# Where the value products are written and which engine takes which small step, in a one-core attention and two-expert layer on Trainium2

## The reference

```python
h = _layernorm(x) * (1 + ca) + sa
x = x + ga * attn(h, w_dq, w_uq, w_dkv, w_ukv, w_out)      # softmax(q k^T / 4 + causal mask) v
h = _layernorm(x) * (1 + cb) + sb
scores = softmax(h @ Wg.T); top = argmax(scores)             # two experts
out0 = gelu(h @ W0a.T + b0a) @ W0b.T + b0b                   # exact gelu
out1 = relu(h @ W1a.T + b1a) @ W1b.T + b1b
x = x + gb * where(top == 0, out0, out1)
```

## Time and profile before

| | us |
|---|---|
| median of 3 runs | 596.92 (595.57 to 600.63) |
| profiled execution | 593.84, its span 592.1 |
| PE busy | 515.4 (87% of the span) |
| DVE busy | 480.8 (81%) |
| ACT busy | 366.5 (62%) |
| POOL busy | 311.9 (53%) |

### The profile page before, as it was taken

How to read it: one execution, slowest core, us unless ns; L and a number is a source line. 1 busy time by engine, 2 the same in 40 slices (tenths; PEclk the granted TensorE clock), 3 DMA queues, 4 the chain that set the end, 5 groups by cost and what they waited for, 6 DMA issues and landing times.

```text
span 592.1 us, 14257 instructions
## 1 busy us (share of the span) xinstructions
PE 515.4 (87%) x4912; PEld 446.2 (75%) x4912; DVE 480.8 (81%) x949; ACT 366.5 (62%) x521; POOL 311.9 (53%) x300
## 2 busy tenths in 40 slices
PE   4534685989999999999999999999999999999974
PEld 4424463788888988888888888788988898888874
DVE  3538163779999899989898989999899999887573
ACT  1524464858585866667676858585766667676320
POOL 6235232455656665755646565656665665552441
PEclk9856598899999999999999999999999999999998
DMA  8835453262707080716244351708080615210100
GB/s 246 206 46 76 50 74 75 52 95 37 128 18 145 2 161 3 121 42 90 71 68 93 50 111 31 130 7 154 0 152 13 108 39 91 55 39 2 37 19 18
DMA packets 43802, 43.74 MB, mean 74 GB/s; under 512 B 5344, under 2 KB 40800, under 8 KB 43760
## 3 DMA queue, kind: packets, MB, share of 16 engines
q1 hardware_dynamic: 43760, 43.19, 39.1%
HBM read 13.39 MB, written 4.23 MB: 30 GB/s over the span
## 4 chain that ended last, share of the span: by engine, by line
PE 49%; DVE 19%; DMA 10%; issue 9%; SPq 5%; POOL 3%; ACT 3%; DVEq 0%; POOLq 0%; ACTq 0%
DMA qs<-parts_q 8%; PE ps_s L382 6%; DVE mx L933 6%; PE ps_t L401 5%; PE ps_o L419 3%; PE ps_a L333 3%; PE ps_t L405 3%; SPq L282 3%; PE ps_a L334 3%; PE ps_a L335 3%; PE ps_c L333 3%; PE ps_c L335 2%; PE ps_c L334 2%; PE ps_o L333 2%; POOL xs L1186 2%
## 5 line engine op out<-in xcount | busy, mean ns | idle before, releaser
L794 ACT ACTIVATE score_rows<-ps_s 128x1024 f32<-128x1024 f32 x96 | 98.8, 1030 | 79.3 <-PE ps_s L382 66.2
L1246 POOL TENSOR_SCALAR_AFFINE_SELECT score_rows<-score_rows 128x512 f32<-128x512 f32 (+1 forms) x96 | 80.0, 834 | 110.4 <-ACT score_rows L794 109.8
L933 DVE TENSOR_REDUCE mx<-score_rows 128x4 f32<-128x1024 f32 (+1 forms) x96 | 114.6, 1210 | 5.7 <-POOL score_rows L1246 5.5
L806 ACT ACTIVATE p<-ps_t 128x1024 f32<-128x1024 f32 x96 | 98.5, 1026 | 17.9 <-PE ps_t L405 17.3
L382 PE MATMUL ps_s<-ks,qs 96*128 96x256 bf16 (+1 forms) x512 | 63.3, 260 | 33.2 <-DMA qs<-parts_q 29.7
L382 PEld LDWEIGHTS ps_s<-ks,qs 96*128 96x128 bf16 x512 | 37.0, 103 | 47.9 <-DMA qs<-parts_q 23.2
L1186 POOL TENSOR_TENSOR xs<-z,xs 128x512 f32<-128x512 f32 (+1 forms) x16 | 34.9, 2182 | 68.7 <-DVE z L1022 68.7
L401 PE MATMUL ps_t<-qs,ks 99*128 99x256 bf16 (+1 forms) x512 | 61.1, 254 | 11.0 <-DMA qs<-mx_rows 10.3
L401 PEld LDWEIGHTS ps_t<-qs,ks 99*128 99x128 bf16 x512 | 38.8, 101 | 17.5 <-DMA qs<-mx_rows 6.3
L405 PE MATMUL ps_t<-past_b,ident_b 128*128 128x256 bf16 (+1 forms) x192 | 46.0, 322 | 0.0
L1234 POOL TENSOR_TENSOR hid_lo<-hid,hid_hi 128x512 fp32r<-128x512 f32 x32 | 42.8, 1350 | 4.8 <-DVE hid_hi L1092 4.8
(11 more groups left out here) (166 smaller groups left out, 1631.4 us busy)
## 6 DMA issues: line engine op xcount, KB each, us to landing
qs<-parts_q SPq DMA_DIRECT2D x96, 128.0 KB, 4.0
ks<-parts_k SPq DMA_DIRECT2D x96, 128.0 KB, 4.7
xs<-x SPq DMA_DIRECT2D x16, 256.0 KB, 4.1
gates<-gates_scratch SPq DMA_DIRECT2D x16, 256.0 KB, 4.5
out<-xs SPq DMA_DIRECT2D x16, 256.0 KB, 2.9
p<-wmod SPq DMA_DIRECT2D x1, 1024.0 KB, 6.7
p<-waT SPq DMA_DIRECT2D x1, 1024.0 KB, 9.1
p<-wmod SPq DMA_DIRECT2D x1, 512.0 KB, 5.9
```

Source lines behind the costliest of these rows:

```text
L794: act.activation(score_rows[c % 2][:], ps_s[:], ACT.Copy).then_inc(scores_out, 1)
L806: act.activation((p0, p1)[tile][:, h0:h0 + n, :], ps_t[:].rearrange("p (h s) -> p h s", h=n), ACT.Exp, scale=SCALE).then_inc(exp_done, 1)
L933: dve.tensor_reduce(dst, score_rows[c % 2][:].rearrange("p (h k) -> p h k", h=n), AX_X, ALU.max).then_inc(max_done, 1)
L1246: pool.affine_select(out=diag, in_=diag, compare_op=ALU.is_ge, fill=NEG, base=0, pattern=[[0, n], [-1, P]], channel_multiplier=1).then_inc ...
```

## The change

- `values` computes all four groups in one piece, into `ps_t` (each group 256 columns), after the last exponentials of the batch; `values_copy` reads it there in two halves, both at the end of ACT's step (before: the second half was second in the next step). The first `st_chunk` of the next batch waits for these copies. The memset of `ps_o` at the start goes. `turn_values(at(3), 0)` now names other users of `ps_o`.
- `choose_expert` reads the first logit straight from PSUM and copies only the second; `second` comes from a comparison "less than" of its own instead of from `first`.
- `relu` moves from DVE to ACT, with the same waits; `relu(at(4), 2)` stands ahead of `v_copy`, `attn_hi` and the first `exponentials`, `relu(at(4), 3)` ahead of the first `scores_copy`.
- On SP `stack_q(_, 2)` moves from the head of the next step to behind `stack_k(at(0), 0)`, and `load_maxima` goes ahead of `load_gates`.
- POOL gets a wait for the end of `split_maxima`, `leave_to_split(at(1))`, between `q_third` and `k_third`.

The diff, cut to its core:

```diff
@@ sync step
-                stack_q(at(1), 2)
                 stack_q(at(0), 0)
                 stack_q(at(0), 1)
                 stack_k(at(0), 0)
+                stack_q(at(0), 2)
+                load_maxima(at(1))
                 load_gates(at(2))
-                load_maxima(at(1))
                 stack_k(at(0), 1)
@@ tensor
-                "GT": ((logit_rows_ready, 1, 1),), "GX": ((logits_ready, 1, 1),),
+                "GT": ((logit_rows_ready, 1, 1),), "GX": ((choice_ready, 2, 2),),
...
                 if c == 0:
                     pe.wait_ge(maxrows_in, 16 * (b.n + 1))
+                    wait(pe, o_ready, 2 * b.n)
...
+            def values(b):
+
+                if b.off:
+                    return
+                pe.wait_ge(v_ready, b.n + 1)
+                pe.wait_ge(exp_done, CH * (b.n + 1))
+                for g in range(4):
+                    for n in range(4):
+                        h = 4 * g + n
+                        dst = ps_t[32 * n:32 * n + HD + 1, g * S:(g + 1) * S]
+                        pe.matmul(dst, v[b.parity][:, 0, h, :], p0[:, h, :], start=True, stop=False)
+                        mm = pe.matmul(dst[:, P:S], v[b.parity][:, 1, h, :], p1[:, h, :], start=False, stop=True)
+                    if g % 2 == 1:
+                        mm.then_inc(pv_done, 1)
...
                 st_chunk(at(2), 5)
-                values(at(2), 0, ("DN0", at(4)), ("UP3", at(4)), ("V", at(1)))
                 s_chunk(at(1), 5)
-                values(at(2), 1)
                 expand_k(at(0), ("CKV", at(0)))
                 up(at(3), 0, ("Q", at(0)), ("T2", at(3)))
-                values(at(2), 2, ("PVa", at(2)))
-                values(at(2), 3)
+                values(at(2))
                 up(at(3), 1, ("DN1", at(4)), ("T1", at(0)))
@@ scalar
+            def relu(b, u):
+
+                if b.off:
+                    return
+                act.wait_ge(up_done, 4 * b.n + u + 1)
+                act.wait_ge(lo_gelu_ready, 2 * b.n + u - 1)
+                act.wait_ge(hid_hi_ready, 4 * b.n + u - 1)
+                for n in range(2):
+                    ins = act.activation(hid32[:, u - 2, n, :], BANK[f"UP{u}"][:, n * S:(n + 1) * S], ACT.Relu,
+                                         bias=bias_a[:, 2 * u + n:2 * u + n + 1])
+                ins.then_inc(relu_done, 1)
...
                 gelu(at(4), 0)
-                values_copy(at(3), 1)
                 maxima_rows(at(2))
                 gelu(at(4), 1)
+                relu(at(4), 2)
                 v_copy(at(1))
                 attn_hi(at(3))
                 exponentials(at(2), 0)
+                relu(at(4), 3)
                 scores_copy(at(1), 0)
...
                 scores_copy(at(1), 5)
+                k_first(at(0))
                 values_copy(at(2), 0)
-                k_first(at(0))
+                values_copy(at(2), 1)
@@ vector
-                dve.tensor_copy(logits[:], BANK["GX"][:, 0:2 * TT].rearrange("p (t e) -> p t e", e=2)).then_inc(logits_ready, 1)
+                pair = BANK["GX"][:, 0:2 * TT].rearrange("p (t e) -> p t e", e=2)
+                dve.tensor_copy(logits[:, :, 1], pair[:, :, 1]).then_inc(logits_ready, 1)
                 dve.wait_ge(logits_ready, b.n + 1)
-                dve.tensor_tensor(first[b.parity][:], logits[:, :, 0], logits[:, :, 1], ALU.is_ge).then_inc(first_ready, 1)
-                dve.wait_ge(first_ready, b.n + 1)
-                dve.tensor_scalar(second[b.parity][:], first[b.parity][:], -1.0, 1.0, ALU.mult, ALU.add).then_inc(choice_ready, 1)
+                dve.tensor_tensor(first[b.parity][:], pair[:, :, 0], logits[:, :, 1], ALU.is_ge).then_inc(choice_ready, 1)
+                dve.tensor_tensor(second[b.parity][:], pair[:, :, 0], logits[:, :, 1], ALU.is_lt).then_inc(choice_ready, 1)
@@ gpsimd
+            def leave_to_split(b):
+
+                if b.off:
+                    return
+                pool.wait_ge(max_split, 4 * (b.n + 1))
...
                 q_third(at(0))
+                leave_to_split(at(1))
                 k_third(at(0))
                 hidden_low(at(3), 0)
```

More of the change, by code:

```diff
@@ L186, in block_kernel @@
             "z2_ready t2_done g32_ready g_hi_ready g_lo_ready".split())
-        gate_done, logit_rows_ready, gate_turned, logits_ready, first_ready, choice_ready = (sem(n) for n in
-            "gate_done logit_rows_ready gate_turned logits_ready first_ready choice_ready".split())
+        gate_done, logit_rows_ready, gate_turned, logits_ready, choice_ready = (sem(n) for n in
+            "gate_done logit_rows_ready gate_turned logits_ready choice_ready".split())
         up_done, gelu_done, relu_done, hid_hi_ready, lo_gelu_ready, lo_relu_ready = (sem(n) for n in
@@ L210, in block_kernel @@
         BANK = dict(T1=ps_a, Q=ps_c, CKV=ps_b, K=ps_b, V=ps_o, MT=ps_c, OT0=ps_o, OT1=ps_b, AT=ps_b, OP=ps_c, T2=ps_c,
-                    GT=ps_a, GX=ps_b, UP0=ps_c, UP1=ps_a, UP2=ps_c, UP3=ps_o, DN0=ps_o, DN1=ps_a, PVa=ps_o, PVb=ps_o)
+                    GT=ps_a, GX=ps_b, UP0=ps_c, UP1=ps_a, UP2=ps_c, UP3=ps_o, DN0=ps_o, DN1=ps_a)
         LAGS = 4
@@ L406, in st_chunk @@
                 mm.then_inc(st_done, 1)
-            def values(b, g, *users):
+            def values(b):
                 if b.off:
                     return
[L412 to L421, removed]
+                pe.wait_ge(v_ready, b.n + 1)
[8 more added lines that the diff above has]
+                        mm.then_inc(pv_done, 1)
             def turn_values(b, t, *users):
@@ L603, in _ @@
             pe.wait_ge(consts_ready, 6)
-            pe.wait_ge(blank, 4)
+            pe.wait_ge(blank, 3)
             pe.wait_ge(z1_ready, 1)
@@ L625, in step @@
                 st_chunk(at(2), 0)
-                up(at(4), 3, ("V", at(1)), ("OT0", at(3)), ("PVb", at(3)), ("PVa", at(3)), ("DN0", at(5)))
+                up(at(4), 3, ("V", at(1)), ("OT0", at(3)), ("DN0", at(5)))
                 project_out(at(3), ("UP2", at(4)), ("MT", at(2)))
@@ L685, in values_copy @@
                     return
-                act.wait_ge(pv_done, 4 * b.n + 2 * half + 2)
+                act.wait_ge(pv_done, 2 * b.n + half + 1)
                 wait(act, ot_done, 2 * b.n)
-                act.activation(oT[:, 2 * half:2 * half + 2, :], BANK["PVa"][:].rearrange("p (g s) -> p g s", g=2), ACT.Copy).then_inc(o_ready, 1)
+                act.activation(oT[:, 2 * half:2 * half + 2, :], ps_t[:, half * 512:(half + 1) * 512].rearrange("p (g s) -> p g s", g=2), ACT.Copy).then_inc(o_ready, 1)
             def second_expert(b, t):
@@ L694, in second_expert @@
                 act.wait_ge(dn_done, 4 * b.n + 2 * t + 2)
-                act.wait_ge(choice_ready, b.n + 1)
+                act.wait_ge(choice_ready, 2 * (b.n + 1))
                 wait(act, out_ready, b.n)
@@ L763, in v_copy @@
                 act.wait_ge(v_done, b.n + 1)
-                wait(act, pv_done, 4 * (b.n - 1))
+                wait(act, pv_done, 2 * (b.n - 1))
                 act.activation(v[b.parity][:, :, :, 0:HD], BANK["V"][:].rearrange("p (t h e) -> p t h e", t=TT, h=NH), ACT.Copy).then_inc(v_ready, 1)
@@ L799, in exponentials @@
                 act.wait_ge(st_done, CH * b.n + c + 1)
-                wait(act, pv_done, 4 * (b.n - 1) + (2, 1, 2, 4, 3, 4)[c])
+                wait(act, pv_done, 2 * (b.n - 1) + (1, 1, 1, 2, 2, 2)[c])
                 if b.first and c == 0:
@@ L915, in _ @@
                 dve.memset(v[n][:, :, :, HD:HD + 1], 1.0).then_inc(blank, 1)
-            dve.memset(ps_o[:], 0.0).then_inc(blank, 1)
             stats(Batch(0, 0, NB), 0)
@@ L1123, in step @@
                 first_stats(at(0))
-                relu(at(4), 2)
                 attn_low(at(3))
                 hidden_high(at(4), 2)
-                relu(at(4), 3)
                 gate_copy(at(4))
```

17 lines of the change are left out of this document (3 added, 14 removed).

## The result

The changed kernel takes 624.75 us in the median of four runs (621.07 to 626.86), the kernel before 596.9: 4.5% slower, ratio 1.045 with a 95% interval of 1.038 to 1.052. The forecast was 597.4 us and the range ended at 607.

What follows compares the result with a forecast made beforehand. Two nearly equal loops were taken to bound a step: PE's work, and split, maxima rows, SP's list, DMA. Regular steps +1.2, third step +0.6, last step −1.3 gave +0.5 us: 597.4 us from 596.92, range 586 to 607.

Steps and rivals of the forecast that it cites:

- 0.4 us later: ACT, regular step: maxima rows are copied only after second value copy, table load and gelu, so their DMA starts 0.4 us later.
- PE takes over from there: Regular step: DVE, relieved of about 2.9 us, bounds no more; PE's 0.2 us wait for the split goes.
- 0.2 us sooner for the last issue: SP's list: behind the maxima one 0.58 us issue leaves and the gates' 0.36 us enters, so the last issue comes sooner.
- The landing: Time from the last part's issue to its arrival for `s_chunk` 0: taken as 3.65 us, possibly 0.7 us later.
- Rival C: Slower: the late k part lands 0.7 us later than a q part would; 607 us, chance 0.06.
- Third step: Filling: PE's 5.10 us idling for the maxima goes, but `s_chunk` 0 comes about 0.6 us later; +0.6 us.
- Last step: Emptying: relu on ACT starts sooner, so the gate's copy on DVE is ready at about 577.0; −1.3 us.
- rival D: Slower: the relus on ACT need a table load each, two more of 1.28 us; 628 us, chance 0.02.
- rival B: Slower: ACT held behind `relu` 2, which waits for GpSimd's `hidden_low`; 604 to 611 us, chance 0.20.
- lower bound: DVE, new choice: `second` was bounded by 0.17 and 1.20 us; 0.2 us was taken, a gain of 1.0 us.
- rival A: Faster: DVE's room pulls work before the split forward, SP's last DMA lands sooner; 583 to 589 us, chance 0.27.
- The merged bursts: PE: four value groups in one piece take 2.90 instead of 3.05 us, a gain of 0.15 us.

Runs made afterwards that it cites:

- gelu_first: The changed kernel with gelu 0 moved to the end of ACT's step before, ahead of the two value copies: 603.9 us, ratio 1.014.
- sp_q_only: The kernel before with only the third part of q issued behind the first of k, gates still ahead of the maxima: 606.3 us, ratio 1.022.
- sp_only: The kernel before with SP's whole new list alone (third q part moved, maxima ahead of gates): 609.0 us, ratio 1.020.
- relu_back: The changed kernel with relu back on DVE in its old places: 624.75 us, ratio 1.047.
- hold_only: The kernel before with GpSimd's wait for the split between q_third and k_third alone: 594.3 us, ratio 0.995.
- choice_relu: The kernel before with relu on ACT and the choice read from PSUM, all else as before: 594.9 us, ratio 0.996.
- loads_last_relief: The kernel before with the last k and q parts issued ahead of the store and the load of x, relu on ACT, new choice: 582.9 us, ratio 0.981.
- sp_maxima_only: The kernel before with load_maxima ahead of load_gates and nothing else: 627.4 us, ratio 1.055.

## Why the prediction was wrong

**What failed first is a dependency, not a size.** The working followed ACT correctly from the second copy over the table load and the gelu to the maxima rows, and gave the maxima "0.4 us later". It has the gelu end 2.8 us after the values, and it ended 2.9 us after them (320.92 and 323.83). But the prediction has PE's transposition done by then ("PE takes over from there"), although its bank is that of `up` 0 and must be read by that same gelu. Measured, PE stood idle for 1.37 us and began `turn_maxima` 0.14 us after the gelu's end. By the prediction's own numbers the transposition could not start before 310.9, 0.8 us behind the row. PE's idling, with a term of its own in each step, was never in the sum. It also pushes back everything behind: `turn_values`, `up` 2, and the maxima's DMA. One line moved (gelu_first) takes 21 of the 28 us back.

**SP's list** was the second step that failed. "0.2 us sooner for the last issue" was right: counted from `turn_maxima`, the last part is issued 5.03 us later instead of 5.28 in the mean of ten steps. The landing was mis-sized. I took 3.65 us, the shortest of those ten steps before, whose mean is 3.96; in the changed kernel it was 4.84 in the mean and 5.39 in the step shown. Rival C named this mechanism, with 0.7 us more for the landing, and the means differ by 0.9. I gave it a chance of 0.06. Two things were not in the sum at all: the maxima land later behind the early q part, which PE waits for in gelu_first and sp_q_only, and 256 KB of gates between the maxima and the last part delay that part. sp_only put the price of the whole list at 12.8 us.

**The size of the step.** Of the 1.89 us that a step grew, 1.1 are PE's wait ahead of `turn_maxima` and 0.6 lie between it and `s_chunk` 0. The rest is the balance of the lower clock and of PE's slightly shorter work.

**The clock** was not in the sum. It stayed at the upper level in the regular steps before, with waits of at most 1.5 us. In the changed kernel it fell in four of the eleven steps. Each of these took 1.4 to 1.7 us more than the step of 33.6 us that had a wait of 2.09 us and kept its clock.

**Third step.** The 5.10 us wait was expected to go and `s_chunk` 0 to come 0.6 us later. The SP rows and PE rows of that step, first of the kernel before where the earlier trace rows lacks them:

```profile
83.62 1.83 SPq L282 DMA_DIRECT2D ks<-parts_k  x3
...
90.80 0.78 SPq L271 DMA_DIRECT2D qs<-mx_rows  x1
...
94.31 0.55 SPq L282 DMA_DIRECT2D qs<-parts_q  x1
```

```profile
98.57 0.62 PE L382 MATMUL ps_s<-ks,qs 96*128 96x128 bf16 x8 [0.63 <-DMA qs<-parts_q]
```

And of the changed kernel:

```profile
85.29 1.83 SPq L282 DMA_DIRECT2D ks<-parts_k  x3
...
87.81 0.77 SPq L271 DMA_DIRECT2D qs<-mx_rows  x1
88.62 0.42 SPq L260 DMA_DIRECT2D gates_scratch<-gates  x1
93.97 0.36 SPq L263 DMA_DIRECT2D gates<-gates_scratch  x1
...
96.42 0.55 SPq L282 DMA_DIRECT2D ks<-parts_k  x1
```

```profile
93.82 1.04 PE L402 MATMUL ps_t<-qs,ks 99*128 99x128 bf16 x8 [3.75 <-DMA qs<-mx_rows]
...
101.84 1.01 PE L382 MATMUL ps_s<-ks,qs 96*128 96x128 bf16 x8 [3.57 <-issue]
```

The wait for the maxima shrank only to 3.75 us. The maxima were issued 3.0 us sooner (87.81 against 90.80), but behind the q part PE could use them 6.0 us after their issue instead of 3.3. `s_chunk` 0 came at 101.84 instead of 98.57, 3.3 us later. Of these, 1.7 were lost before (the first k parts go at 85.29 instead of 83.62). The other 1.6 stand against the 0.6 of the sum. Counted from those k parts the round trip began 1.45 us later (2.1 in the sum), and it took 0.45 us longer. The last issue behind it came 1.46 us sooner (1.4 in the sum). The landing, of which the sum took no account here, took 5.4 us instead of 4.3.

**Last step.** −1.3 us was expected. The idle time ahead of `turn_gate` fell from 1.86 to 1.07 us, −0.8:

```profile
607.75 0.25 PE L559 MATMUL ps_b<-ident,logit_rows 2*128 2x2 f32 x2 [1.07 <-DVE logit_rows L1066]
```

**What was right.** relu on ACT is as long as on DVE, 471 and 472 ns beside 479, without a table load of its own (rival D is refuted):

```profile
L802 ACT ACTIVATE hid<-ps_c,bias_a 128x256 f32<-128x256 f32 x20 | 8.4, 471 | 20.5 <-PE ps_c L335 12.3 <-POOL hid_lo L1236 8.2
```

It did wait behind GpSimd's `hidden_low` (8.2 us, in four of the steps) and held the v copy, as drawn in the prediction, but PE had other waits by then, and relu_back shows that the place costs nothing here; rival B is refuted as the cause. The Trainium skill (ScalarE: Activation LUTs, Rules for kernel authors) speaks for VectorE with a figure for bf16. For float32 from PSUM the rows show no difference in length. The new choice took 150 ns for `second`, just under the lower bound. That bound's row was misread: at 541.48 GpSimd was not idle but in a 128x2 instruction of 0.70 us from 541.03 on. The instruction took the same 0.17 us at 516.26 and 580.02, with GpSimd idle, so the number stands. DVE was busy for 84% of the regular steps (268.81 of 320 us), near the 85% forecast. GpSimd's wait was free (hold_only). That DVE's relief would shorten nothing while SP's chain closes the step was right as well (choice_relu, 0.996), and the part of rival A that DVE's room shortens the step became true only when the last issue was made sooner (loads_last_relief). The merged bursts are real, four groups in 2.76 us of PE (318.16 to 320.92) where 2.90 were predicted, but they gave no time that can be told from noise.

## What to carry to other kernels

When a step is moved on one engine, look up who waits for it by way of a shared bank, not only who reads its result. Here the line that names the bank's last user held most of the loss, 21 of 28 us. On a DMA queue, look at what stands between one urgent transfer and the next: a 256 KB load for which no wait shows in these tables cost 5.5% between the maxima and the last parts. In the regular steps it cost nothing that could be seen ahead of the maxima or behind the parts. And relief for a full engine is worth nothing until the wait that closes the step is gone: the same two edits gave 1 us before the list was put right and 7 us after.

## What was not expected of the hardware

In the changed kernel, waits of PE of 2.04, 2.32, 2.00 and 2.16 us ahead of `s_chunk` 0 were followed by a stretch at the lower clock, and one of 2.09 us was not. The length of this wait alone does not decide it. In relu_back waits of 1.93 and 1.96 us were followed by such a stretch and waits of 2.08 and 2.11 us were not (another of 2.08 was), and in sp_maxima_only one of 1.85 us was and the 2.89 us of the step shown was not. What else decides it no run here separates.

The time of one 128 KB part from its issue to the matmul that waited for it varies from step to step. In the mean of ten steps it was 3.96 us before (a q part last, 3.65 to 4.24), 4.92 us in sp_maxima_only (a q part, with the gates behind the maxima, 3.91 to 5.92) and 4.84 us in the changed kernel (a k part, 4.23 to 5.39). How much of this is what else is in the queue and how much the part's kind was not separated.

sp_maxima_only loses more than the whole new list, and the rows show where. Its last part is issued 5.86 us after `turn_maxima`, and 5.06 in sp_only, because the q part still follows the last k part. It lands no later (4.92 against 5.14 us). And the clock is 0.94 in the mean of the regular steps against 1.00 in sp_only.
